# A four-layer recurrence over eight groups and a dense expert stage: four groups go through all layers first, and their dense stage is woven into the recurrence of the other four

## What is computed

```
x  = x + layers(adapter(x, ids))
x  = x + sparse(dense(x, gating, shared_gate))

for each of the 4 layers:
    u, z   = split(norm(x) @ W_in.T)           # 256 channels each; u through a 4-tap convolution and silu
    dt,B,C = split(u @ W_x.T)                  # 16 states; dt = softplus(dt @ W_dt.T + b)
    for each token:  h = exp(dt*A) * h + dt*B*u ;  y = sum over states of h*C
    x      = ((y + u*Dp) * silu(z)) @ W_out.T + x
dense:  sum over e of w_e * (silu(h @ Wg_e) * (h @ Wu_e)) @ Wd_e      # 9 experts (one shared), 512 wide
sparse: two best experts by logits, rank within each expert, gelu(disp @ w_gate) @ w_down
```

## Time and profile before

| what | us |
|---|---|
| median of 3 runs (lowest, highest) | 2933.65 (2931.76, 2934.94) |
| the profiled execution | 2935.85 |
| its span, from first to last instruction | 2934.1 |
| VectorE busy | 2104.9 |
| TensorE busy | 2515.8 |
| GpSimd busy | 1780.1 |
| ScalarE busy | 1456.5 |
| first input term of the recurrence, last one | 123.3, 1961.5 |
| dense stage, first residual sum | 1977.9 |

### The profile page before, as it was taken

One profiled execution on the slowest core, in us unless ns is written; L12 is line 12 of the kernel. 1 busy time (PEld: TensorE's weight loads), 2 busy tenths in 40 slices (PEclk: granted clock), 3 DMA queues, 4 the chain that ended last, 5 costly groups with the idle time before them and its releaser, 6 DMA issues. The chain is left out here.

```text
span 2934.1 us, 27727 instructions
## 1 busy us (share of the span) xinstructions
PE 2515.8 (86%) x6470; PEld 1112.9 (38%) x6470; DVE 2104.9 (72%) x2075; ACT 1456.5 (50%) x2337; POOL 1780.1 (61%) x1090
## 2 busy tenths in 40 slices
PE   5588888888888888888888888869999999999586
PEld 3233333333333333333333333324444444444264
DVE  4399999999999999999999999972333333333221
ACT  2366657666666665666566667632222222222222
POOL 3278887888888788888888887861022202221266
PEclk9798999999999999989999999999999999999798
DMA  7334533543453344345434533516000000000154
GB/s 204 139 128 179 201 127 144 194 170 127 170 197 139 136 185 186 127 157 196 154 128 174 205 127 142 195 61 220 8 15 8 15 7 11 25 8 1 45 111 70
DMA packets 130514, 354.33 MB, mean 121 GB/s; under 512 B 21716, under 2 KB 85410, under 8 KB 97570
## 3 DMA queue, kind: packets, MB, share of 16 engines
q1 hardware_dynamic: 116770, 342.46, 32.1%
q0 software_dynamic: 11264, 7.98, 1.8%
q10 hardware_dynamic: 2432, 3.38, 0.3%
HBM read 330.34 MB, written 23.99 MB: 121 GB/s over the span
## 5 line engine op out<-in xcount | busy, mean ns | idle before, releaser
L683 POOL TENSOR_TENSOR gg<-hh,Ct 128x1024 f32<-128x1024 f32 x512 | 1205.0, 2356 | 336.2 <-DVE hh L598 322.4
L598 DVE TENSOR_TENSOR_SCAN hh<-dA,psdB 128x1024 f32<-128x1024 f32 x512 | 1170.7, 2287 | 59.4 <-ACT dA L543 6.1
L385 PE MATMUL psY<-gg,ident 128*128 128x512 f32 x2048 | 1024.4, 636 | 128.0 <-POOL gg L683 127.7
L543 ACT ACTIVATE dA<-dt,Acur 128x508 f32<-128x508 f32 x1024 | 664.6, 707 | 14.9 <-DVE hh L598 14.4
L385 PEld LDWEIGHTS psY<-gg,ident 128*128 128x128 f32 x2048 | 390.9, 200 | 689.8 <-issue 420.6
L592 DVE TENSOR_TENSOR psdB<-psU,Bt 128x1024 f32<-128x1024 f32 x512 | 617.6, 1206 | 36.8 <-ACT psU L522 36.8
L1051 DVE TENSOR_TENSOR ac<-sg,d_bank 128x512 f32<-128x512 f32 x288 | 198.1, 688 | 514.0 <-PE d_bank L901 496.8
L948 ACT ACTIVATE sg<-d_bank 128x512 f32<-128x512 f32 x288 | 171.9, 597 | 534.6 <-PE d_bank L897 521.3
L811 POOL TENSOR_TENSOR xw<-x1T,wbc 128x512 f32<-128x512 f32 x72 | 74.9, 1041 | 568.1 <-PE d_bank L901 563.8
L897 PE MATMUL d_bank<-x1T,wgu 128*128 128x512 f32 x576 | 296.6, 597 | 1.9 <-DMA wgu<-in_Wu 1.9
L901 PE MATMUL d_bank<-xw,wgu 128*128 128x512 f32 x576 | 295.5, 595 | 0.0
(11 more groups left out here) (149 smaller groups left out, 1887.1 us busy)
## 6 DMA issues: line engine op xcount, KB each, us to landing
Bt<-rows SPq DMA_DIRECT2D x128, 1024.0 KB, 6.0
Ct<-rows SPq DMA_DIRECT2D x128, 1024.0 KB, 4.7
wcur<-taps_l SPq DMA_DIRECT2D x33, 512.0 KB
disp<-zrow SPq DMA_DIRECT2D x16, 528.0 KB, 12.1
dx<-disp SPq DMA_DIRECT2D x16, 528.0 KB, 6.5
wcur<-in_W_inT SPq DMA_DIRECT2D x33, 128.0 KB
diag<-diags_l SPq DMA_DIRECT2D x33, 128.0 KB
ad_gb<-in_gb SPq DMA_DIRECT2D x32, 128.0 KB, 3.3
```

Of the source, the lines that this page charges most:

```text
L385: ins = pe.matmul(psY[:, :], lhsT=ident[:, :], rhs=gg[k % NGB][:, j, :], start=False, stop=(k % NK == NK - 1 and j == 1))
L543: ins = act.activation(dA[k % NDA][:, j, :, 1:T], dt[p][:, c, :, 1:T], ACT.Exp, scale=Acur[p][:, s:s + 1])
L598: dve.tensor_tensor_scan(out=hh[k % NHB][:, :, :].rearrange("p c t -> p (c t)"), data0=dA[k % NDA][:, :, :, :].rearrange("p c q t -> p (c ...
L683: pool.tensor_tensor(gg[k % NGB][:, :, :], hh[k % NHB][:, :, :], Ct[:, s:s + 2, :], ALU.mult).then_inc(prod, 1)
```

## The change

`mamba_phase` becomes `wave_phase`, written out without loops.

1. **Order of the groups.** ROUND = 4: iteration t is for group `t // 16 * 4 + t % 4` and layer `t // 4 % 4`. So groups 0 to 3 have all four layers behind them after iteration 15.
2. **Dense stage of groups 0 to 3 inside.** From FIRST = 15 on, each iteration carries nine of the 144 pieces (NDF * NF = 16 iterations): gate, up and down products on TensorE at steps G_AT, U_AT, D_AT, a copy of each gate to `f_sg` and one silu over nine of them on ScalarE, the product `f_ac` on VectorE, the scaling `f_xw` on GpSimd. Their weights are loaded in a ring of three. The gate and the up product use the two banks of `psdB1`, so from iteration 14 on the input term has one buffer only, and waits for the scan before it. `dense_phase` keeps groups 4 to 7 and the routing of all eight.
3. **Input term from SBUF.** `place_dtu` and `psU` are gone; VectorE reads `dtu` (now two buffers) and `Bt`, both in SBUF.
4. **Steps by pairs of states.** Steps alternate between the two halves: step k is for half k % 2 and pair k // 2. `psY` has two banks, one for each half, and is copied once in an iteration (`sums`, at ScalarE's step 5) and gated once (1024 columns). `Bt` and `Ct` are rings of four pairs, loaded pair by pair.
5. **Three input terms by GpSimd in iterations 0 to 13.** For steps 4, 9 and 13 GpSimd makes the product into `f_sg` (`give`), ScalarE copies it into `psdB` (`move_given`), and VectorE makes none.
6. **One sum for two in eight steps, from iteration 15 on.** In the steps of PAIRED GpSimd adds the two states of `gg` (`gg<-gg`, 512 columns), and TensorE multiplies once.
7. **Residual in the projection.** TensorE adds `h_res` by one more identity product, and ScalarE writes the sum to `h_res`; GpSimd's `residual` is gone. The clearing of `disp` moves into the recurrence, too.

The core of the diff:

```diff
-NK = NS // 2
-NSTEP = NH * NK
+NSTEP = NS
+ROUND = NG // 2
+FIRST = NL * ROUND - 1
+GIVEN = {4: 0, 9: 5, 13: 8}
+G_AT = [-9, -8, -6, -5, -4, -3, -2, -1, 3]
+U_AT = [6, 8, 9, 11, 12, 14, 15, 19, 20]
+D_AT = [10, 10, 11, 13, 14, 18, 18, 21, 22]
+PAIRED = [0, 1, 2, 5, 8, 13, 14, 15]
...
-                def place_dtu(t, c):
-                    act.wait_ge(dtu_ok, CR + t + 1)
-                    at_least(act, dbu, CR + NSTEP * (t - 1) + NK * (c + 1))
-                    act.activation(psU[c][:, :], dtu[:, c, :], ACT.Copy).then_inc(placed, 1)
...
-                    dve.tensor_tensor(dB[k % NDB][:, :, :], psU[c][:, :].unsqueeze(1).broadcast_to([128, 2, TOK]), Bt[:, s:s + 2, :], ALU.mult).then_inc(dbu, 1)
+                    if assisted(i, k):
+                        return
+                    b, free = (k % NDB, n + 1 - NDB) if i < FIRST - 1 else (0, n)
+                    at_least(dve, scan, free)
+                    dve.tensor_tensor(dB[b][:, :, :], dtu[i % 2][:, c, :].unsqueeze(1).broadcast_to([128, 2, TOK]), Bt[:, s % NPR, :, :], ALU.mult).then_inc(dbu, 1)
...
+                def act_product(n):
+                    dve.wait_ge(sg_ok, n // NB + 1)
+                    dve.wait_ge(upped, n + 1)
+                    at_least(dve, downed, n - 1)
+                    dve.tensor_tensor(ac[n % 2][:, :], sg[:, n % NSLG, :], psU, ALU.mult).then_inc(acted, 1)
...
+                def give(i, k):
+                    n, c, s = NSTEP * i + k, k % NH, k // NH
+                    pool.wait_ge(b_ld[s % NPR], 16 * (NS // 2 // NPR * i + s // NPR + 1))
+                    at_least(pool, moved, helped(n) - 1)
+                    pool.tensor_tensor(given[helped(n) % 2], dtu[i % 2][:, c, :].unsqueeze(1).broadcast_to([128, 2, TOK]), Bt[:, s % NPR, :, :], ALU.mult).then_inc(gave, 1)
...
+                    if i >= FIRST and k in PAIRED:
+                        ins.then_inc(half, 1)
+                        pool.wait_ge(half, len(PAIRED) * (i - FIRST) + PAIRED.index(k) + 1)
+                        ins = pool.tensor_tensor(gg[k % NGB][:, 0, :], gg[k % NGB][:, 0, :], gg[k % NGB][:, 1, :], ALU.add)
```

More of the change, by code:

```diff
@@ L296, in mamba_phase @@
[L296 to L316 removed]
+        sg = sb("f_sg", [128, NSLG, TOK])
@@ new lines, in sum_states, with out_projection @@
+                def sum_states(i, k):
+                    n = NSTEP * i + k
+                    pe.wait_ge(prod, n + 1)
+                    last = 1 if i >= FIRST and k in PAIRED else 2
+                    for j in range(last):
+                        ins = pe.matmul(psY[:, k % NH, :], lhsT=ident[:, :], rhs=gg[k % NGB][:, j, :], start=False, stop=(k >= NSTEP - NH and j == last - 1))
+                    ins.then_inc(red, 1)
+                def out_projection(t):
+                    pe.wait_ge(ygated, t + 1)
+                    pe.wait_ge(wfree, W["out", t])
+                    pe.matmul(psW[:, :], lhsT=ident[:, :], rhs=flat(group(t)), start=True, stop=False)
@@ new lines, in _ @@
+                transposes(1)
+                for i in range(NIT):
+                    for k in range(NSTEP):
+                        if k > 0:
+                            sum_states(i, k)
+                        for n in stream(D_AT, i, k):
+                            down(n)
+                        for n in stream(U_AT, i, k):
+                            up(n)
+                        if k == T_AT and i >= FIRST - 1 and (i - FIRST + 1) % NF == 0 and (i - FIRST + 1) // NF < NDF:
+                            transpose_x((i - FIRST + 1) // NF)
+                        for n in stream(G_AT, i, k):
+                            gate(n)
+                        for what in PE_AT.get(k, ()):
+                            if what in PRE and i + 1 < NIT:
+                                pre(i + 1, what)
+                            if what == "out" and i > 0:
+                                out_projection(i - 1)
+                            if what == "transposes" and i + 2 < NIT:
+                                transposes(i + 2)
+                        if k == 0:
+                            skip(i)
+                            sum_states(i, k)
@@ L575, in _ @@
+                            if what == "sums" and i > 0:
+                                copy_sums(i - 1)
+                        decay(i, k)
+                copy_sums(NIT - 1)
+                added(NIT - 1)
             @block.vector
             def _(dve):
-                for sm in (dbu, scan, stat, moments):
-                    dve.sem_inc(sm, CR)
                 for b in range(NDA):
                     ins = dve.memset(dA[b][:, :, :, 0:1], 0.0)
-                ins.then_inc(zeroed, 1)
@@ L701, in dense_phase @@
+                gate(NIT - 1)
 def dense_phase(nc, A, K, out):
@@ L753, in at_least, with posts, sums @@
                 eng.wait_ge(sm, v)
-        def loop(eng, first, body, last):
-            first()
-            body(0, 0, False, True)
-            with eng.Fori(0, NG // 2 - 1) as j:
-                body(2 * j + 1, 1, True, True)
-                body(2 * j + 2, 0, True, True)
-            body(NG - 1, 1, True, False)
-            last(NG - 1, 1)
+        def posts(h, r, at):
+            return [2 * h + j for j in range(2) if 2 * h + j < NG - 1 and r == P_AT[j] + at]
+        def sums(g):
+            return h_res[:, G * g:G * (g + 1), :]
         with nc.Block() as block:
```

895 lines of the change are left out of this document (490 added, 405 removed).

## The result

The changed kernel takes 3254.65 us (median of 4 runs, 3253.28 to 3255.93), the kernel before 2933.16 beside it: a ratio of 1.1096 with a 95% interval of 1.1076 to 1.1115. The forecast had the sign and not the size: +122 us were expected, +321 measured, and the time lies above the range. One execution of the kernel before, in the round of the experiments e9, e10 and e11, took 6048 us at a granted clock of 0.45 and is left out of their ratios, which rest on its two others.

A forecast was written before the change was run, and what follows sets the result against it. VectorE was taken to bound the recurrence and TensorE the dense stage. The recurrence going from 1833 to 2326 us (+493) and the dense stage's -372 took 2935.85 to 3057, by the median 3055 us; 8-in-10 range 2800 to 3220.

The forecast's parts named there:

- The dense stage: Behind the recurrence: four groups' products, 370 us, and transposes, about 2 us, leave this TensorE-bound part, -372 us.
- The mechanism: Recurrence: with both input-term inputs in SBUF, VectorE and GpSimd take turns, so their times add up; +493 us.
- rival C: Recurrence: VectorE is passed over repeatedly when GpSimd has two rows queued; 3201 us in all, chance 0.12.
- Rival B: Recurrence: the exclusion hardly costs and VectorE stays the limit; 2675 us in all, chance 0.18.
- rival D: Recurrence: half the exclusion is hidden, price 0.5 us per input term; 2800 us in all, chance 0.05.
- The price of an input term: Recurrence: one input term of 1024 columns adds 1.0 us to the time VectorE and GpSimd share.
- The first half: Iterations 0 to 13: GpSimd's 52.6 us, 13 input terms at 1.0 and 1.4 idle make 67 us, ends 62 and 72.
- The given terms: Iterations 0 to 13: three input terms fewer bring VectorE from 57.27 to 53.4 us; ScalarE stays under 50.
- Iteration 14: The iteration without GpSimd's help: 43.9 + 1.76 + 16 = 62 us, 60 to 66.
- The second half: Iterations 15 to 31: GpSimd's 58.9 us, 16 for input terms and 3 added make 78 us, ends 70 and 84.
- The wait for TensorE: Iterations 15 to 31: VectorE's dense product waits for up products behind delayed sums; covered by the upper end, 84 us.
- TensorE's sum: Iterations 15 to 31: TensorE saves eight products and gains 27 and one, 43.7 + 20 x 0.857 = 60.8 us.

The follow-up runs named there:

- e9: Changed kernel with VectorE's dense product left out for groups 0 to 3 (a one-column memset stands for it): 3084.07 us, ratio 1.0505.
- e10: Changed kernel without VectorE's dense product, and from iteration 14 GpSimd waits before each product for the next input term: 3068.2 us, ratio 1.0451.
- e11: Changed kernel, GpSimd waiting for next input term from iteration 14, no given terms or pairs, input term reading dtu from PSUM in iterations 0-13: 2999.79 us.
- the order by hand: Changed kernel; from iteration 14 GpSimd waits, before each product with C, for the next step's input term: 3213.62 us, ratio 1.0943.
- The best kernel: Changed kernel, GpSimd waiting for next input term, no given terms or pairs, dtu in PSUM in first half, up and down products before sums: 2919.69 us.
- three edits: Changed kernel with no given terms, no pairs, and GpSimd waiting for the next input term from iteration 14, all together: 3090.25 us, ratio 1.0523.

## Why the prediction was right in sign and wrong in size

**The dense stage, -372 us: right.** It measured -368.

**The mechanism: right.** Both inputs in SBUF make the input term and GpSimd's rows take turns. The signs came: the mean of the input term is 2.30 us, GpSimd's product 2.81, and no input term is over 3.44, so VectorE was never passed over (rival C, whose 3201 us comes nearest to the time, but by a mechanism that did not occur). The kernel before with that one operand moved loses 303 us. Rival B is shown wrong by it, rival D by the distances.

**The price of an input term, 1.0 us: right.** GpSimd's row grew by 0.98.

**The first half, 67 us: close, with two errors in it.** The shared sum with 0.98 is 52.6 + 12.7 = 65.3, so that idle places take 3.0 us by it, not 1.4; the window above shows GpSimd idle for 68.27 - 64.50 = 3.8. By the whole instruction, as the Trainium skill (SBUF — State Buffer, Who interferes with whom) has it, the sum was 68.3, and 68.28 was measured, yet the row shows a price of 0.98 and not 1.21: the rest is idle time, and the agreement is luck. The given terms were counted as a plain gain for VectorE at no cost to ScalarE ("ScalarE ... still under 50, at nothing"). That step failed, though it is hidden here: a mean share of busy time says nothing of a queue in which a move stands ahead of a decay. Without turns the help lengthens an iteration by 4.3 us, with them by 2.2.

**Iteration 14, 62 us: too low.** The two distances around it are 74.09 and 77.12 where 65 and 68 follow from the forecast: 18 us. With the order by hand they are 70.53 and 68.61, so most of it is again GpSimd ahead of the input term, from the single buffer on.

**The second half, 78 us: the step that failed.** I wrote "78 (74.9 + 3)" and put its upper end at 84; it measured 89.3. The term is "I add 3": it should have been 14. The prediction described the very thing, GpSimd's product starting in the dense product's 0.61 us, and then reckoned the dense product as hidden under GpSimd's time because VectorE's own sum, 64.0, was less than 74.9. Two engines that exclude each other at one instruction and feed each other at the next can't be bounded by the larger sum. In most steps here scan, GpSimd's product and input term stand one behind another, 5.90 us, with the dense product beside GpSimd's product and GpSimd idle for 3.54. Without the dense product the distance is 78.43. From first scan to first scan, iterations 15 to 31 took 1499 us where 1326 were forecast, 173 more; iterations 0 to 13 took 17 more and iteration 14 took 15 more. The kernel before had taken 1842 and not 1833 us there, which leaves some 197 by which the forecast of the difference was short.

**The wait for TensorE, "inside the upper end": too low.** It is small in the change (35 us in 900) only because the turns cover it: with no turns at all it is 9.3 us an iteration. As soon as the turns are ordered it takes their place (163 us), which is why the repair that I expected to bring some 165 to 195 us brought 41.

**TensorE's sum, 60.8 us: not tested** as a bound. The best kernel has 8 products more and TensorE busy for 738.16 / 800 x 77.21 = 71.2 of 77.2 us, so its amount of work may be the next bound; no run here tells.

## What to carry to other kernels

Before an operand moves from PSUM to SBUF, look at what GpSimd does beside the instruction: in this kernel a VectorE row with two SBUF inputs and a GpSimd row added up, and both showed the wait as busy time, so a mean duration above the shortest one is the sign to look for. When two engines take turns, don't take the larger of their sums; follow one step as a chain and see who asks first after each signal. And repair such a chain as a whole: three edits that gave 24, 20 and 41 us singly gave 164 together, and a wait removed alone was replaced by another almost of its size.

## What the runs showed of the hardware

A turn can be decided by hundredths of a microsecond: at 1544.42 against 1544.45 GpSimd had it and the input term took 3.41 us. And even GpSimd's smallest rows wait their turn: the one of 128 x 4 that makes `vare` took 1.18 us at 1540.84, while the input term of 1538.94 had its turn (it ended at 1541.97), and 0.21 where none ran, in the kernel with the order by hand:

```profile
1540.84 1.18 POOL L784 TENSOR_TENSOR vare<-mv,eps 128x4 f32<-128x4 f32 x1
```

```profile
1535.22 0.21 POOL L784 TENSOR_TENSOR vare<-mv,eps 128x4 f32<-128x4 f32 x1
```
